# A fused embedding, attention and expert kernel: the turning of the router's exponentials moved from after the first unit of a turn to the end of the turn before, with two copies of q issued by SyncE

## The reference, cut to what matters

```python
h = concat([cls_token, patches(x) @ W_lin.T + b_lin, txt])      # 32 x 325 x 192, f32
h = h + attention(layernorm(h))        # 12 heads of 16, rms-normed and rotated q and k, causal softmax
n = layernorm(h)
shared = (silu(n @ sg) * (n @ su)) @ sd                          # 192 -> 384 -> 192
p = sigmoid(n @ router_w + routing_bias)                         # 3 experts
s, idx = top_k(p, 2);  s = s / s.sum()
h = h + shared + sum over the 2 chosen of s_e * ((silu(n @ g_e) * (n @ u_e)) @ d_e)
```

## Time and profile before

| | |
|---|---|
| median of 3 runs | 1612.2 us (1610.06 to 1612.52) |
| profiled execution | 1611.11 us, its span 1609.1 us |
| TensorE busy | 1577.0 us, 98% |
| VectorE, ScalarE, GpSimd busy | 75%, 55%, 26% |
| mean granted TensorE clock | 0.995 |
| DMA engines' mean busy tenths | 1 to 2 of 10 after the start |

### The profile page before, as it was taken

The page is one execution under the profiler, slowest core; times in us unless marked ns, Lnnn a source line. Parts: engine busy times, 40 slices in busy tenths (PEclk is TensorE's granted clock), DMA queues, the critical chain, the costliest instruction groups (busy, mean ns, idle before and its releaser), DMA issues.

```text
span 1609.1 us, 46516 instructions
## 1 busy us (share of the span) xinstructions
PE 1577.0 (98%) x16632; PEld 1487.4 (92%) x16632; DVE 1204.8 (75%) x3383; ACT 882.5 (55%) x1896; POOL 410.4 (26%) x647
## 2 busy tenths in 40 slices
PE   6899999999999999999999999999999999999999
PEld 6699999999999999999999999999999999998998
DVE  6777787777877777877778877778877778877765
ACT  4555554556645565555566555566555566555552
POOL 1332321232311323212233212323212323212320
PEclk8999999999999999999999999999999999999999
DMA  6211221111211112111111111111111111111110
GB/s 218 74 39 59 69 69 36 48 61 62 69 48 45 54 61 69 55 44 43 49 53 57 47 42 39 50 50 57 51 39 39 48 50 57 53 38 33 36 33 13
DMA packets 75381, 86.80 MB, mean 54 GB/s; under 512 B 12720, under 2 KB 64328, under 8 KB 75208
## 3 DMA queue, kind: packets, MB, share of 16 engines
q1 hardware_dynamic: 64776, 65.45, 11.9%
q10 hardware_dynamic: 10560, 20.74, 3.9%
HBM read 32.44 MB, written 12.51 MB: 28 GB/s over the span
## 4 chain that ended last, share of the span: by engine, by line
PE 81%; DVE 11%; DMA 3%; issue 2%; ACT 1%; SPq 1%; POOL 0%; DVEq 0%; POOLq 0%
PE ps L426 74%; PE ps L429 5%; DMA kt<-kt 3%; DVE rotated L1166 2%; DVE xt L1106 1%; DVE o L1075 1%; PE ps L626 1%; DVE stats L1095 1%; DVE qk_split L1171 1%; DVE rotated L1138 1%; DVE kt L1178 1%; DVE h L1199 1%; SPq L368 0%; DVE rms L1150 0%; DVE mean_var L1100 0%
## 5 line engine op out<-in xcount | busy, mean ns | idle before, releaser
L426 PE MATMUL ps<-xt,wf 64*128 64x326 f32 x6912 | 598.0, 316 | 0.0
L426 PEld LDWEIGHTS ps<-xt,wf 64*128 64x128 f32 x6912 | 536.9, 186 | 3.4 <-issue 0.8
L426 PE MATMUL ps<-w_down_s,ht 128*128 128x192 f32 (+1 forms) x2304 | 413.8, 329 | 0.0
L426 PEld LDWEIGHTS ps<-w_down_s,ht 128*128 128x128 f32 (+1 forms) x2304 | 351.0, 174 | 14.5 <-issue 0.2
L1052 DVE SCALAR_TENSOR_TENSOR gated<-tanh_g,ps 128x326 f32<-128x326 f32 x384 | 188.7, 491 | 117.6 <-ACT tanh_g L827 116.4
L820 ACT ACTIVATE rows<-h,rstd 128x192 f32<-128x192 f32 (+2 forms) x279 | 151.1, 564 | 211.4 <-POOL rstd L1022 206.6
L838 ACT ACTIVATE probs<-ps 128x792 f32<-128x792 f32 (+1 forms) x384 | 254.3, 663 | 22.6 <-PE ps L426 22.5
L1011 POOL TENSOR_TENSOR probs<-probs,causal 128x512 f32<-128x512 f32 x192 | 228.9, 1192 | 132.0 <-ACT probs L838 132.0
L827 ACT ACTIVATE tanh_g<-ps 128x326 f32<-128x326 f32 x384 | 170.2, 443 | 157.7 <-PE ps L426 156.2
L1005 POOL TENSOR_TENSOR probs<-probs,causal 69x140 f32<-69x140 f32 x192 | 89.2, 465 | 480.0 <-ACT probs L838 479.9
L1058 DVE TENSOR_TENSOR ht<-gated,ps 128x326 f32<-128x326 f32 x384 | 190.1, 495 | 13.2
(11 more groups left out here) (105 smaller groups left out, 2012.2 us busy)
## 6 DMA issues: line engine op xcount, KB each, us to landing
kt<-kt SPq DMA_DIRECT2D x384, 40.8 KB, 1.8
x_s<-in_xp ACTq DMA_DIRECT2D x40, 384.0 KB, 3.2
qt<-qt SPq DMA_DIRECT2D x132, 81.5 KB, 1.9
residual<-h SPq DMA_DIRECT2D x31, 288.0 KB, 2.4
out<-o SPq DMA_DIRECT2D x32, 192.0 KB
qt<-qt ACTq DMA_DIRECT2D x60, 81.5 KB, 2.8
kept_rows<-embed_rows SPq DMA_DIRECT2D x44, 96.0 KB, 1.7
h<-kept_rows SPq DMA_DIRECT2D x30, 95.2 KB
```

Source lines behind the costliest of these rows:

```text
L426: return nc.tensor.matmul(dst, lhs, rhs, start=first, stop=last)
```

## The change

It has these parts: the turning goes from after unit 0 of the next turn to the end of the same turn on TensorE, as three full 128 x 128 transposes into bank 1; the exponential goes ahead of the last copy of q on ScalarE; `route_sum` goes ahead of the gate of unit 0 on VectorE; `score(0)` waits for `route_seen` in place of `route_exp`, and unit 2 takes over the wait for the last group of k; the first two copies of q are issued by SyncE, behind a wait of its own, ahead of those of k.

```diff
@@ -68,7 +68,7 @@
 N2_BANK = [3, 0, 1]
 VALUE_BANK = [2, 3, 0]
 KEEP_BANK = [6, 7, 2, 3, 6, 7]
-XT_BANK, YT_BANK, EMBED_BANK, ROUTER_BANK, ROUTE_BANK, PROJ_BANK = 6, 4, 2, 0, 7, 0
+XT_BANK, YT_BANK, EMBED_BANK, ROUTER_BANK, ROUTE_BANK, PROJ_BANK = 6, 4, 2, 0, 1, 0
 SPLIT_PARTS = len(SPLIT_AT) - 1
 START_EMBED_BANK, START_XT_BANK = [EMBED_BANK, 4], [XT_BANK, 4]
 START_STEP_BANK = [0, 6]
@@ -389,6 +389,9 @@
                 if T:
                     load_hidden(b0, at)
                 if L:
+                    sp.wait_ge(qt_kept.sem, qt_kept.at(b1, 1))
+                    for m in range(2):
+                        double_q(m)
                     for g in range(GROUPS):
                         double_group(g, b1, g > 0)
                 if N:
@@ -486,7 +489,7 @@
                 elif k == 2:
                     if A:
                         pe.wait_ge(qt_kept.sem, qt_kept.at(b + 1, GROUPS))
-                    pe.wait_ge(route_seen.sem, route_seen.at(b, 1))
+                        pe.wait_ge(kt_kept.sem, kt_kept.at(b + 1, GROUPS))
                 else:
                     pe.wait_ge(h_ready.sem, h_ready.at(b, k - 2))
                 for j in range(BLOCKS):
@@ -502,7 +505,7 @@
                 if n:
                     pe.wait_ge(exp_done.sem, exp_done.at(b, n))
                 elif F:
-                    pe.wait_ge(route_exp.sem, route_exp.at(b - 1, 1))
+                    pe.wait_ge(route_seen.sem, route_seen.at(b - 1, 1))
                 if n % 2 == 0:
                     pe.wait_ge(qk_doubled[p].sem, qk_doubled[p].at(b, 48))
                 score_products(n, 0)
@@ -650,14 +653,11 @@
                                   j + x == 0, j + x == BLOCKS)
                 last.then_inc(router_done.sem, 1)
 
-            def route_turn(b, A):
+            def route_turn(b):
 
                 pe.wait_ge(route_exp.sem, route_exp.at(b, 1))
-                if A:
-                    pe.wait_ge(kt_kept.sem, kt_kept.at(b + 1, GROUPS))
                 for t in range(TILES):
-                    last = mm(ps[:, ROUTE_BANK, t * P:t * P + R_COLS], route_e[0:H, t * P:(t + 1) * P], ident[0:H, 0:R_COLS],
-                              True, True)
+                    last = turned(ps[:, ROUTE_BANK, t * P:(t + 1) * P], route_e[:, t * P:(t + 1) * P], P)
                 last.then_inc(route_turned.sem, 1)
 
             def down(e, t, b, L=True, A=True):
@@ -677,8 +677,6 @@
                 for k in range(UNITS):
                     if F:
                         unit(k, b3, at, D, A)
-                        if k == 0:
-                            route_turn(b3, A)
                     if A:
                         score(k, b2, F)
                 if A:
@@ -740,6 +738,8 @@
                 if L:
                     for n in range(4, 2 * GROUPS):
                         qk_turn(n, b1, at, N)
+                if A:
+                    route_turn(b2)
 
             def start_qk_turn(n, b):
 
@@ -803,6 +803,7 @@
             for n in range(4, 2 * GROUPS):
                 start_qk_turn(n, 1)
             router(0)
+            route_turn(0)
             pe.wait_ge(s_ffn_high, SPLIT_PARTS)
             pe.wait_ge(s_ffn_split, SPLIT_PARTS)
             turns(pe, turn)
@@ -836,6 +837,12 @@
                 else:
                     dst, src = probs[:, p:p + 2, P_MID:P_COLS], ps[:, bank:bank + 2, 0:COLS1]
                 nc.scalar.activation(dst, src, ACT.Exp, scale=ATTN_SCALE / ROOT_GAIN ** 2).then_inc(exp_done.sem, 1)
+
+            def route_up(b):
+
+                act.wait_ge(router_done.sem, router_done.at(b, 1))
+                nc.scalar.activation(route_e[0:R_COLS, 0:COLS], ps[0:R_COLS, ROUTER_BANK, 0:COLS], ACT.Exp, scale=-1.0,
+                                     bias=router_bias[:, 0:1]).then_inc(route_exp.sem, 1)
 
             def keep_high(h, dst, bank, turned, b, done):
 
@@ -901,14 +908,10 @@
                         act.wait_ge(qk_turned.sem, qk_turned.at(b1, 2 * g + 1))
                         twice = shaped(ps[:], [[0, 2], [1, COLS]], KEEP_BANK[2 * g] * 512)
                         copy(qt[:, 2 * g:2 * g + 2, :], twice).then_inc(qt_kept.sem, 1)
-                        if g == 0:
-                            act.wait_ge(qt_kept.sem, qt_kept.at(b1, 1))
-                            for m in range(2):
-                                act.dma_start(f32(qt[1 - m:P:2, m, :]), f32(qt[m:P:2, m, :])).then_inc(qk_doubled[m].sem, 16)
-                if A:
-                    act.wait_ge(router_done.sem, router_done.at(b2, 1))
-                    nc.scalar.activation(route_e[0:R_COLS, 0:COLS], ps[0:R_COLS, ROUTER_BANK, 0:COLS], ACT.Exp, scale=-1.0,
-                                         bias=router_bias[:, 0:1]).then_inc(route_exp.sem, 1)
+                        if g == 1 and A:
+                            route_up(b2)
+                elif A:
+                    route_up(b2)
 
             def start_norm1(b):
 
@@ -990,10 +993,8 @@
                 keep_high(j, xt2[:, j, 0, :], N2_BANK[j], n2_turned, 0, xt2_hi)
             start_keep_q(1, 1)
             start_keep_q(2, 1)
-            act.wait_ge(router_done.sem, router_done.at(0, 1))
             act.wait_ge(s_halve, 1)
-            nc.scalar.activation(route_e[0:R_COLS, 0:COLS], ps[0:R_COLS, ROUTER_BANK, 0:COLS], ACT.Exp, scale=-1.0,
-                                 bias=router_bias[:, 0:1]).then_inc(route_exp.sem, 1)
+            route_up(0)
             turns(act, turn)
 
         @block.gpsimd
@@ -1243,12 +1244,13 @@
                     if D:
                         sum_up(6, b3 - 1)
                     sum_up(7, b3 - 1)
+                if F:
+                    route_sum(b3)
                 for k in range(UNITS):
                     if F:
                         gate(k, b3)
                         up(k, b3)
                         if k == 0:
-                            route_sum(b3)
                             for n in range(3):
                                 route_pick(n, b3)
                         elif k == 1:
```

## The result

The changed kernel takes 1619.72 us, the median of 5 runs (1619.05 to 1620.19), against 1611.79 (1606.92 to 1612.52) for the kernel before: a ratio of 1.0055, interval 1.0040 to 1.0071. So it is slower, by 7.9 us in the medians and by about 9 in the ratio, where I had forecast 2.3 us. The profiled execution took 1620.19 us, its span 1618.2, which is 9.1 more than before.

A forecast was written before the change was run, and what follows sets the result against it. TensorE bounds 13 boundaries, k's DMA 17. 13 times +0.10 (0.67 + 0.08 - 0.65), 17 times 0, first +0.6 and last +0.45 sum to +2.35 us: forecast 1614.5, own range 1612 to 1619, overall range 1608 to 1620.

The forecast's parts named there:

- rival 1: Second k transfer of pair 0 lands later behind two q transfers in one queue; 3.4 us on top, 1618; chance 0.20.
- Rival 2: VectorE not caught up by the sixth unit, units wait for `h_ready`; 0.3 in 12 turns, 3.6 us, 1618; chance 0.10.
- What bounds the kernel: TensorE alone after two-tile turns; after one-tile turns the second k transfer of pair 0, which score 0 awaits.
- DMA-set boundaries: 17 turn starts after turns embedding at most one tile, where score 0 waits for k's DMA; forecast cost 17 times 0.
- score 0 still waits for `kt<-kt` in one-tile turns: Sign that the forecast is right: this wait for k's transfer stays and the one-tile turns' length does not change.
- What goes, 0.65 us: Behind unit 0: the six passes of `route_turn` on the lower row half disappear, saving 0.65, between 0.46 and 0.67.
- What comes, 0.67 us: At the turn's end TensorE waits for the exponential, then does three transposes; unit 0 starts 0.67 later, ends 0.61 and 0.75.
- Score 0 and `route_seen`, 0.08: Score 0 now waits for VectorE's sums and `route_sum`, due just as unit 0 ends; 0.08 added, between 0 and 0.18.
- The first boundary, 0.6: Before turn 1: unit 0 starts 1.45 later, less 0.65 to 0.95 for the six passes; +0.6.
- The last boundary: Before the last turn, which has no score: unit 0 +1.1 us, less 0.65 for the six passes; +0.45.
- The doubling: SyncE issues q's first copies ahead of k's, so the second k issue begins at 618.6 instead of 618.27; priced at no cost.
- Rivals 3 and 4: Exponential hidden behind transposes, 1608; or q stops competing with k, shortening one-tile starts by at most 0.28, 1609.7; together 0.12.

The follow-up runs named there:

- e8: Kernel before, with each load of `h` split into a multiple of 16 rows and the rest; 1608.38 us, ratio 0.9975.
- e1: Changed kernel, with the three transposes moved past the loop's end and behind the waits of unit 0; 1614.06 us, ratio 1.0021.
- e2: Changed kernel, with exponential's wait and transposes moved past the loop's end but ahead of unit 0's waits; 1611.61 us, one run.
- e5: Changed kernel, with four more long-satisfied waits of TensorE behind the three transposes; 1624.88 us, one run.
- e6: Kernel before, with four long-satisfied waits at the end of TensorE's turn; 1612.98 us, one run.
- e4: Kernel before, with only the first two copies of q issued by SyncE ahead of those of k; 1613.58 us, ratio 1.0006.
- e3: Kernel before, with three full 128 x 128 transposes in the old place behind unit 0 instead of six passes; 1610.20 us, ratio 0.9992.
- e7: Kernel before, with q's first copies issued by SyncE and the exponential ahead of the last copy of q; 1612.98 us, ratio 1.0005.

## Why the prediction was wrong, step by step

The measured 1619.72 us lies just inside the range of 1608 to 1620 on record, but that is luck: the forecast's own range ended at 1619, the rest was there for rivals 1 and 2, and neither happened.

**What bounds the kernel: right.** The DMA-set boundaries could take a delay and did: their turns grew by under 0.1 us on average where the two-tile ones grew by 0.50. e8 shows that what held k's transfer there was the loads of `h` ahead of it. The sign I gave, that score 0 still waits for `kt<-kt` in one-tile turns, did not come in most: unit 0 is 1.15 later and not 0.67, which uses the wait up. Of the 14 waits and 5.8 us there is left

```profile
PEld ps L429 <- DMA kt<-kt: 1.3, 4, 0.7
```

That sign should have depended on the size of the delay.

**What goes, 0.65 us: right.** The piece of the chain that begins with unit 0 is 20.92 against 21.51, 0.59 less; it isn't cut at quite the same instruction. From the first matmul of unit 0 to the last of unit 11 it is 18.37 against 19.02 us in the two-tile turns, 0.65 less.

**What comes, 0.67 us: wrong, it was 1.15.** The step that failed is the one that goes from the last transpose to unit 0, for which I allowed 0.10 (0.04 to 0.17) and which took 0.57 (0.90 from the first transpose to unit 0, less 0.33 for the three). I counted the array's instructions and the wait, and nothing for the sequencer, since in the trace of before those waits and the loop's end cost nothing. They cost nothing because TensorE's sequencer was ahead, and my own new wait took that lead away (e1, e2 and e5 against e6). The prediction asked what is queued behind a new wait on SyncE; it did not ask so on TensorE. Where no loop ends the step was nearly right: after turn 30, in code without a loop, the changed kernel's TensorE shows

```profile
1543.82 0.60 PE L629 MATMUL ps<-ident_r,qk_split 128*128 128x128 f32 x6
1544.60 0.55 PE L432 MATMUL ps<-ident,route_e 128*128 128x128 f32 x3 [0.18 <-ACT route_e L844]
1545.07 1.17 PE L429 MATMUL ps<-xt,wf 64*128 64x326 f32 x12
```

and the kernel before at the same place

```profile
1535.28 0.61 PE L626 MATMUL ps<-ident_r,qk_split 128*128 128x128 f32 x6
1535.82 1.63 PE L426 MATMUL ps<-xt,wf 64*128 64x326 f32 x18
```

From the last groups' first transpose to unit 0 it is 1.25 us against 0.54: 0.71, where 0.67 was forecast. In the loop it is 1.68 (673.92 to 675.60), so 1.15 more.

**Score 0 and `route_seen`, 0.08: not seen.** With unit 0 half a microsecond later still, VectorE was done in time: score 0 follows unit 0 by 1.43 us, no more than the 1.46 I had taken for its products. After a two-tile turn the sum is thus 1.15 - 0.65 = 0.50 and not 0.10.

**The first boundary, 0.6: too small.** Unit 0 starts 1.14 later (I had said 1.45; the router itself began 0.44 earlier in that execution, 73.67 against 74.11), but the 0.65 to 0.95 of the six passes did not come back, since the clock rose later: unit 0 to unit 1 is still 2.95 us (76.97 to 79.92) against 3.15 (75.83 to 78.98), and the next unit lost 0.45. That makes about 1.3 in place of 0.6. The last boundary came as forecast: 1.1 us later, 0.65 back in its units.

**The doubling, and rivals 1 to 4.** Second k transfer of pair 0 (rival 1): no wait for it in any two-tile turn, and e4 shows no cost. Rival 2 (VectorE late at unit 6): no wait of TensorE for `ht` there. Rivals 3 and 4 would have made it faster, and the wait for the exponential was there and as long as forecast, 0.29 us of idle each:

```profile
PEld ps L429 <- ACT qt L814: 6.2, 11, 0.6
PEld ps L432 <- ACT route_e L844: 3.2, 11, 0.3
```

These are the waits of TensorE's weight loads in two-tile turns (160 to 720 us: total us, times, longest). The second row is the wait I had forecast, 11 times 0.29. The first row, 11 times 0.56, is the one I had not, under the name of an instruction that was not waited for: L814 is the copy of q, and in the stretch without a loop unit 0 starts while that copy still runs. No rival had the loss in it.

## What to carry to other kernels

Before you put a real wait in front of work on a busy engine, list what its sequencer has to do between the wait and the next long instruction: loop end, register work, each wait. Put the real wait behind the dear items of that list. Here the loop's end was the dear one (0.35 of 0.36 us a turn); going past the satisfied waits too gained 0.01. And when a profile puts idle time behind a real wait down to something that was long done, look at the sequencer's own lines before you believe the name.

## What the runs showed of the hardware that I had not expected

A loop's end on TensorE is worth 0.34 us when its sequencer has no lead, with a branch of 208 ns in it, and a satisfied wait about 0.06 us (e5). With a lead the loop's end is free (before) and so are waits until the lead is used up: four of them cost 0.05 us after a two-tile turn and 0.22 after a one-tile turn (e6). Three full 128 x 128 f32 transposes between stretches of 64-row matmuls cost 0.65 us over the turn, as much as six passes on one row half (e3), while at the edge of a stretch of full-row work unit 0 begins 0.44 after the first of them (e1). Where the new wait left TensorE idle for a part of the first boundary, at the lower clock level, the granted clock stayed there through the stretch (0.50 against 0.71 from 75 to 80 us), in every kept trace with that wait and in none without. What caused the one long k transfer in the profiled executions of e4, e7 and e8 (2 to 3 us more in one turn) stays open; their run to run spread, 6 to 8 us, may come from it, which is not shown.
